# Turning the queries on GpSimd ahead of the token lists, in a fused attention and mixture-of-experts kernel

## The chip, the cores and the metric

One core of a Trainium2 chip runs the whole layer in one launch. The metric is the device time of one execution in microseconds. Engines are named as the profile names them: PE (TensorE), DVE (VectorE), ACT (ScalarE), POOL (GpSimd), SP (SyncE, which only issues DMAs here).

## What is computed

```python
xn = layernorm(x)                                   # x: (8, 256, 256) f32, so 2048 tokens of 256
q, k, v = xn @ Wq + bq, xn @ Wk + bk, xn @ Wv + bv  # 16 heads of 16
q, k = rope(q), rope(k)                             # x*cos + rotated(x)*sin
attn = softmax(causal(q @ k.T / 4)) @ v             # per head, 256 x 256
w, ids = top_k(softmax(xn @ gate.T), 6)             # 64 experts, 6 per token
routed = sum over the 6 of w * down_e(silu(g_e) * u_e)   # FFN width 176
shared = down_s(silu(g_s) * u_s)                    # width 352, all tokens
out = x + attn @ Wo + bo + routed + shared
```

## The kernel before

The program is written engine by engine; the order on each engine is the order of the code, and engines meet only through semaphores. It has four stages, and PE goes through them in this order.

1. Layer norm, transposes, V and router logits (`xn_transpose`, `mix`), then sixteen projections `project(n)` (L1109): four spans of 512 tokens, and in each span two halves of the queries, then two halves of the keys. ACT copies every result out with its bias (`projected`, L560, semaphore `qkv_ok`). Between projections PE computes the ranks of the router, which DVE needs for the slots of every token (L788 to L834; L834 raises `tables_ok`, L788 raises `chosen`).
2. The shared experts on all tokens (`shared_up`, `shared_down`), and beside them the token lists: for each of 16 tiles of tokens DVE writes 12 one-hot tables in fp16 (`one_hot`, L838, two buffers, so at most two tiles ahead) and PE multiplies them (`list_tokens`, L1147). DVE then copies the finished list to `idx_all` (L953, `idx_ok`).
3. The routed experts: 128 tiles of 128 slots, two experts of 64 slots each in a tile, taken two tiles at a time. POOL gathers the rows of a tile by an indirect DMA (`gather`, L450), at most four tiles ahead; PE transposes them (L1168), multiplies up (L1211), transposes (L1222) and multiplies down (L1238). DVE copies the weights of a tile's second expert (`up_copy` L927, `down_copy` L934) and forms the hidden values (L869). SP loads the weights of an expert once its place in a ring of eight is free (L359 to L362).
4. Attention, with the routed results gathered and added beside it.

The change concerns the rotation of queries and keys. Q and K lie in SBUF as pieces: piece n belongs to span n // 2, even n are the queries, odd n the keys. A piece is 128 partitions x 2 halves x 512. It takes nine steps: two products with sin into a spare buffer, two products with cos in place, a subtraction, an addition, a rounded copy, and two differences. Then eight DMAs of 256 KB store it to `qk_rows`, from where stage 4 loads it. In the kernel before, POOL turns the queries (`piece`, L456, steps L481 to L491) and stores queries and keys (L466); DVE turns the keys, one step per pair of tiles in the routed loop (`turn_keys`, L883). All of POOL's steps and stores stand in the routed loop between the gathers, spread evenly by count:

```python
steps = [(n, k) for n in range(PIECES) for k in range(ROPE_STEPS if n % 2 else 0, PIECE_STEPS)]
for r in range(RT):
    gather(r)
    while r >= XB and r % 2 and done < (r - XB + 1) * todo // (RT - 4 * XB) and done < todo:
        piece(*steps[done])
```

Every step of a piece waits for the step ahead of it (`roped`), and the first store of a key piece waits for DVE's ninth step on it (`turned_ok`, L463). There are four spare buffers (`spare`, L230). Number 0 is the space of `raw` and `on`, which the shared experts use for their silu (`gS`, L243), so the first step waits for all shared results (L472). Numbers 1 and 2 lie over router tables, number 3 is free. The fifth and later pieces wait until the stores of the piece four before have landed (`rows_out`, L474 on POOL, L893 on DVE).

Of the kernel before, what the change touches and what calls it, by code (L numbers as in the profile page):

```python
# [35 lines left out]
NT = T // P  # L36
# [12 lines left out]
RT = ((T * TOPK + NE * (GRAIN - 1)) // GRAIN + STRIPS - 1) // STRIPS  # L49
TILES = RT  # L50
XB = 4
# [32 lines left out]
SPAN_T = T // SPANS  # L84
# [7 lines left out]
PIECES = 2 * SPANS  # L92
BUFS = 4
ROPE_STEPS = 9
COPIES = 4
PIECE_STEPS = ROPE_STEPS + 2 * COPIES
# [9 lines left out]
def build(nc, x, wqkv, bqk, bv, bo, wo, wr, wgu, wdn, rope, tri, ident, mask, before, upto, tileno, thr, tok, iota,  # L106
# [7 lines left out]
    with ctx:  # L114
        def sb(name, shape, dt=F32):
            return ctx.enter_context(nc.sbuf_tensor(name, shape, dt))

        def sem(name):
            return ctx.enter_context(nc.semaphore(name))
# [105 lines left out]
        with nc.sbuf_tensor("spare_high", [P, 2, SPAN_T], F32) as spare_high:  # L225
            pass
        raw = sb("raw", [P, 2, S])
        on = sb("on", [P, SB, E])
# [11 lines left out]
        hT = work[0:FP, :, EC * P:(EC + 2) * P].rearrange("p u (k q) -> p u k q", q=P)  # L240
        hS = [[z[:, at * SPAN_T:(at + 1) * SPAN_T] for at in range(2)] + [work[:, u, EC * P:EC * P + SPAN_T]]
              for u, z in enumerate((y.rearrange("p u e -> p (u e)"), freed[0]))]
        gS = [raw[:].rearrange("p u s -> p (u s)"), on[:].rearrange("p s e -> p (s e)")]  # L243
        sg, hid = work[:, :, 4 * P:4 * P + F], work[:, :, 6 * P:6 * P + F]

        wqkv_flat = wqkv_sb[:].rearrange("p c n -> p (c n)")
        own_gu = [wqkv_flat[:, 0:GU].rearrange("p (c n) -> p c n", c=EC),
                  room[:, 1, 0:GU].rearrange("p (c n) -> p c n", c=EC)]
        own_dn = [wqkv_flat[0:FP, GU:GU + DN].rearrange("p (c n) -> p c n", c=2), room[0:FP, 1, GU:GU + DN].rearrange("p (c n) -> p c n", c=2)]
# [26 lines left out]
        tables_ok = sem("tables_ok"); onehot_ok = sem("onehot_ok"); listed = sem("listed"); idx_ok = sem("idx_ok"); dpair = sem("dpair")  # L276
# [50 lines left out]
        order = [(g, k) for g in range(SPANS) for k in range(4)]  # L327
# [107 lines left out]
        @block.gpsimd  # L435
        def _(po):
            po.memset(ones_b[:], 1.0)
            po.memset(ones_c[:], 1.0).then_inc(ones_ok, 1)
            po.memset(v_all[:, :, :, D:2 * D], 1.0).then_inc(pad_ok, 1)
            po.wait_ge(pad_ok, 1)  # L440
            po.memset(work[ROWS[-1]:ROWS[-1] + 1, :, EC * P:EC * P + SPAN_T], 1.0).then_inc(hone_ok, 1)
            po.wait_ge(hone_ok, 1)

            po.wait_ge(c_in_act, 16 * CONSTS)
            for k in range(8):
                a, cs, s = k // 4, k // 2 % 2, k % 2
                last = po.tensor_copy(table_in[:, k], rope_sb[:, s, cs, a, 1::2].unsqueeze(1).to_broadcast([P, H, D // 2]))
            last.then_inc(table_set, 1)

            def gather(r):  # L450
                if r >= XB:
                    po.wait_ge(xt_done, r - XB + 1)
                po.indirect_dma_start(xg[:, r % XB, :], None, xn_rows[:, :],  # L453
                                      bass.IndirectOffsetOnAxis(idx_all[:, r:r + 1], 0)).then_inc(xg_in[r % XB], 16)

            def piece(n, k):  # L456

                g, a, u = n // 2, n % 2, n % BUFS
                q, other = qT[:, g, a], spare[u]
                if k >= ROPE_STEPS:  # L460
                    i, x = (k - ROPE_STEPS) // 2, (k - ROPE_STEPS) % 2
                    if k == ROPE_STEPS:
                        po.wait_ge(turned_ok if a else roped, ROPE_STEPS * (n // 2 + 1))  # L463
                    at = qk_rows.rearrange("(h i x d) a t -> h i d x a t", h=H, i=COPIES, x=2)
                    src = other if i in HIGH_IN[a] else q
                    po.dma_start(at[:, i, :, x, a, g * SPAN_T:(g + 1) * SPAN_T], src[:, x]).then_inc(rows_out[u], 16)  # L466
                    return
                if n or k:
                    po.wait_ge(roped, ROPE_STEPS * (n // 2) + k)
                    po.sem_inc(po_turn, 1)  # L470
                if n == 0 and k == 0:
                    po.wait_ge(sdn_ok, NT)  # L472
                if k == 0 and n >= BUFS:
                    po.wait_ge(rows_out[u], 16 * 2 * COPIES * (n // BUFS))  # L474
                cos, sin = (table[:, a, cs].unsqueeze(1).to_broadcast([P, SPAN_T // S, S]) for cs in range(2))

                def batches(z):
                    return z.rearrange("p (b s) -> p b s", s=S)

                if k < 2:  # L480
                    i = po.tensor_tensor(batches(other[:, k]), batches(q[:, 1 - k]), sin, ALU.mult)  # L481
                elif k < 4:
                    i = po.tensor_tensor(batches(q[:, k - 2]), batches(q[:, k - 2]), cos, ALU.mult)
                elif k == 4:
                    i = po.tensor_tensor(q[:, 0], q[:, 0], other[:, 0], ALU.subtract)
                elif k == 5:
                    i = po.tensor_tensor(q[:, 1], q[:, 1], other[:, 1], ALU.add)
                elif k == 6:
                    i = po.tensor_copy(other.bitcast(F32R), q)
                else:  # L490
                    i = po.tensor_tensor(q[:, k - 7], q[:, k - 7], other[:, k - 7], ALU.subtract)  # L491
                i.then_inc(roped, 1)

            po.wait_ge(qkv_ok, len(order))
            po.wait_ge(tables_in, 1)
            po.wait_ge(idx_ok, 1)
            po.wait_ge(xn_out, 16 * NT)
            steps = [(n, k) for n in range(PIECES) for k in range(ROPE_STEPS if n % 2 else 0, PIECE_STEPS)]
            todo = len(steps)
            done = 0  # L500
            for r in range(RT):
                gather(r)
                while r >= XB and r % 2 and done < (r - XB + 1) * todo // (RT - 4 * XB) and done < todo:
                    piece(*steps[done])
                    done += 1
            assert done == todo

            def rows(t, u):

                for k in range(TOPK):  # L510
                    slot = ROWS_FROM + (TOPK * t + k) * NS // (TOPK * NT)
                    if slot < 0:
                        po.wait_ge(max_ok, slot + AHEAD + 1)
                    else:
                        po.wait_ge(exp_done, slot + 1)
                    if t >= 2:
                        po.wait_ge(dcomb, TOPK * (t - 2) + k + 1)
                    po.indirect_dma_start(yg[u][:, k, :], None, y_rows[:, :],  # L518
                                          bass.IndirectOffsetOnAxis(slot_i[:, t, k:k + 1], 0)).then_inc(yg_in[u], 16)

            po.wait_ge(dn_ok, TILES)
            for s in range(XB):
                po.wait_ge(y_out[s], 16 * (RT // XB))
            for u in range(2):
                rows(u, u)
            for b in range(2, B + 1):
                for s in range(SB):
                    rows(SB * (b - 1) + s, s)
# [936 lines left out]
```

## Time and profile before

| | us |
|---|---|
| median of 3 runs (652.37 to 657.2) | 652.57 |
| the profiled execution | 650.28 |
| its span in the trace | 648.5 |
| PE busy in the span | 621.4 (96%) |
| DVE busy | 437.5 (67%) |
| POOL busy | 321.6 (50%) |

PE's granted clock is full in the whole span. The profiled execution is 1.78 us longer than its span and 2.29 us shorter than the median. In rows of a timeline the columns are the start, the duration, the engine, the line, the operation and what it writes and reads, and in brackets the idle time ahead of it with what ended it. In rows of groups they are the line, the engine, the operation and its shapes, the count, the busy time with the mean in ns, and the idle time ahead.

### The profile page before, as it was taken

How to read it: one execution, taken by the hardware profiler on the slowest of the kernel's cores; microseconds unless marked ns; L12 is line 12 of the kernel's file. 1: busy time of each engine (PE TensorE's matmuls, PEld its weight loads, DVE VectorE, ACT ScalarE, POOL GpSimd, SP SyncE). 2: the span in 40 equal slices, each digit the busy share in tenths (PEclk: the TensorE clock that was granted, in tenths of full speed). 3: DMA queues.
4: the chain of work that ended last, by engine and by line, in shares of the span. 5: the costliest groups of instructions: out<-in, count | busy, mean ns of one | idle time of the engine just before them, and what ended most of it. 6: DMA issues, size and time to landing. Idle time of an engine off the chain costs nothing.

```text
span 648.5 us, 17789 instructions
## 1 busy us (share of the span) xinstructions
PE 621.4 (96%) x4929; PEld 368.7 (57%) x4929; DVE 437.5 (67%) x1364; ACT 306.0 (47%) x798; POOL 321.6 (50%) x340
## 2 busy tenths in 40 slices
PE   7999999999998999999999999999999999999997
PEld 3644455655554555555555555555554666666654
DVE  6768687568665766676665565445446788889865
ACT  3643121024444444444444444445454776777752
POOL 4000000268637766568656776664301766666662
PEclk9999999999999999999999999999999999999999
DMA  9510011138979769995899878995416777877432
GB/s 294 175 37 2 0 34 34 55 85 271 274 243 283 242 190 289 350 304 171 246 310 301 272 230 261 329 271 133 99 50 199 236 218 216 239 218 219 124 105 74
DMA packets 78167, 124.52 MB, mean 192 GB/s; under 512 B 11113, under 2 KB 52618, under 8 KB 78090
## 3 DMA queue, kind: packets, MB, share of 16 engines
q1 hardware_dynamic: 43098, 60.18, 30.4%
q0 software_dynamic: 15872, 46.16, 24.2%
q10 hardware_dynamic: 19120, 17.18, 7.8%
q8 instruction: 45, 0.74, 0.5%
q14 instruction: 32, 0.26, 0.1%
HBM read 85.73 MB, written 37.75 MB: 190 GB/s over the span
## 4 chain that ended last, share of the span: by engine, by line
PE 83%; DVE 5%; DMA 4%; issue 3%; ACT 2%; POOL 2%; DVEq 1%; ACTq 0%; SPq 0%; POOLq 0%
PE pair L1211 23%; PE pair L1238 14%; PE pair L1181 6%; PE pair L1168 5%; PE pair L1116 4%; PE bank L1323 4%; PE bank L1222 3%; PE bank L1195 3%; PE bank L1355 2%; PE pair L1078 2%; PE pair L1278 2%; PE pair L1297 2%; DMA lower<-xn_rows,idx_all 2%; PE pair L1286 2%; DVE negm L980 2%
## 5 line engine op out<-in xcount | busy, mean ns | idle before, releaser
L453 POOL DMA_INDIRECT lower<-xn_rows,idx_all x128 | 139.3, 1089 | 215.0 <-DVE idx_all L953 107.8
L1211 PE MATMUL pair<-space,work 128*64 (+1 forms) x768 | 165.6, 463 | 7.0 <-DVE wqkv_sb L927 3.7
L1238 PE MATMUL pair<-lower,work 88*64 x512 | 122.1, 380 | 1.8 <-ACT lower L614 1.4
L1211 PEld LDWEIGHTS pair<-space,work 128*64 128x64 f32 x768 | 66.8, 137 | 77.7 <-issue 67.2
L869 DVE TENSOR_TENSOR work<-work,pair 128x176 f32<-128x176 f32 x128 | 42.8, 337 | 90.9 <-ACT work L608 90.4
L1238 PEld LDWEIGHTS pair<-lower,work 88*64 88x64 f32 x512 | 69.3, 137 | 50.8 <-issue 20.9
L1211 PE MATMUL pair<-wqkv_sb,work 128*64 128x352 f32 x256 | 89.4, 472 | 0.0
L614 ACT ACTIVATE lower<-pair 128x256 f32<-128x256 f32 x128 | 49.1, 383 | 77.8 <-PE pair L1238 77.8
L518 POOL DMA_INDIRECT wqkv_sb<-y_rows,slot_i x48 | 46.9, 977 | 60.9 <-DVE negm L980 34.0
L980 DVE TENSOR_REDUCE negm<-pair 128x2 f32<-128x256 f32 (+1 forms) x128 | 64.9, 551 | 11.4 <-PE pair L1286 9.9
L659 ACT ACTIVATE pT<-pair 128x768 f32<-128x768 f32 x64 | 51.9, 811 | 42.6 <-PE pair L1309 41.3
L601 ACT ACTIVATE work<-pair 128x256 f32<-128x256 f32 x128 | 42.1, 381 | 62.7 <-PE pair L1168 37.7
L608 ACT ACTIVATE work<-pair 128x176 f32<-128x176 f32 x128 | 41.1, 321 | 57.3 <-PE pair L1211 56.8
L1238 PE MATMUL pair<-space,work 88*64 88x256 f32 x256 | 66.0, 380 | 0.0
L1238 PE MATMUL pair<-wqkv_sb,work 88*64 88x256 f32 x256 | 65.9, 380 | 0.0
L934 DVE COPY space<-lower 88x512 f32 x64 | 35.6, 557 | 31.5 <-issue 30.5
L518 POOL DMA_INDIRECT space<-y_rows,slot_i x48 | 45.8, 954 | 18.4 <-DVE x_all L1024 9.9
L1168 PE MATMUL pair<-id_f,lower 128*128 128x128 f32 x256 | 42.4, 287 | 2.2 <-DMA lower<-xn_rows,idx_all 1.8
L1181 PE MATMUL pair<-space 128*128 128x512 f32 (+1 forms) x96 | 44.4, 596 | 0.0
L622 ACT ACTIVATE work<-bank 88x256 f32<-88x256 f32 x128 | 41.9, 386 | 1.2 <-PE bank L1222 1.2
L1168 PEld LDWEIGHTS pair<-id_f,lower 128*128 128x128 f32 x256 | 27.0, 141 | 27.0 <-issue 24.2
L670 ACT ACTIVATE ring<-qk_all 128x512 fp32r<-128x512 f32 x64 | 39.4, 625 | 1.1 <-ACT lower L614 0.6
(202 smaller groups left out, 1168.6 us busy)
## 6 DMA issues: line engine op xcount, KB each, us to landing
space<-wgu SPq DMA_DIRECT2D x66, 352.0 KB
y_rows<-lower ACTq DMA_DIRECT2D x128, 128.0 KB
qk_all<-qk_rows SPq DMA_DIRECT2D x64, 256.0 KB, 4.2
lower<-wdn SPq DMA_DIRECT2D x64, 176.0 KB
qk_rows<-qk_all POOLq DMA_DIRECT2D x32, 256.0 KB
qk_rows<-space POOLq DMA_DIRECT2D x16, 256.0 KB
xn_rows<-qk_all SPq DMA_DIRECT2D x16, 128.0 KB, 1.8
lower<-xn_rows,idx_all POOLq DMA_INDIRECT x128
```

The costliest lines, as they stand in the source:

```text
L453: po.indirect_dma_start(xg[:, r % XB, :], None, xn_rows[:, :], bass.IndirectOffsetOnAxis(idx_all[:, r:r + 1], 0)).then_inc(xg_in[r % XB], 16)
L518: po.indirect_dma_start(yg[u][:, k, :], None, y_rows[:, :], bass.IndirectOffsetOnAxis(slot_i[:, t, k:k + 1], 0)).then_inc(yg_in[u], 16)
L601: act.activation(xgT[u], bank[u % 2][:, 0:E].rearrange("p (c t) -> p c t", c=EC), ACT.Copy).then_inc(xgT_ok, 1)
L614: act.activation(y[:, u], pair[u % 2][:, 512:512 + E], ACT.Copy).then_inc(y_ok, 1)
L622: act.activation(hT[:, u % 2], bank[2 + u % 2][0:FP, 0:2 * P].rearrange("p (c t) -> p c t", c=2), ACT.Copy).then_inc(hT_ok, 1)
L659: act.activation(pT[:, n % G], pair[1][:].rearrange("p (j k) -> p j k", j=2)[:, :, 0:SPAN], ACT.Exp).then_inc(exp_done, 1)
L869: dve.tensor_tensor(hid[:, u % 2], sg[:, u % 2], pair[u % 2][:, F:2 * F], ALU.mult).then_inc(hid_ok, 1)
L980: last = dve.tensor_reduce(negm[:, qt, m % PAIRS_OF_HEADS], scores[:, :, qt * P:(2 * qt + 1) * P], AX.X, ALU.max, negate=True)
L1168: last = pe.transpose(bank[u % 2][:, c * P:(c + 1) * P], xg[:, u, c * P:(c + 1) * P], id_f[:])
L1181: last = pe.matmul(pair[k % 2][0:ROWS[c], half * SPAN_T:(half + 1) * SPAN_T], wsgu_sb[:, x, at:at + ROWS[c]], xnT[:, TS * span:TS * (span ...
L1211: last = pe.matmul(pair[u % 2][strip, 0:2 * F], xgT[u][:, c, strip], n, start=c == 0, stop=c == EC - 1, skip_group_check=True)
L1238: last = pe.matmul(pair[u % 2][strip, 512:512 + E], hT[:, u % 2, c, strip], n, start=c == 0, stop=c == 1, skip_group_check=True)
```

## The change

POOL now turns and stores all four pieces of queries in one go, before the first gather. Each piece starts when the two projections of its queries have been copied out; the second piece also waits for `tables_ok`, since its spare buffer lies over router tables. Only then comes the wait for the token list and the loop of gathers, in which the 32 stores of the keys are left, one behind every second gather from the 31st on. The silu of the shared experts moves from `raw` and `on` to the projection weights' space. The steps themselves and DVE's part stay.

```diff
-        gS = [raw[:].rearrange("p u s -> p (u s)"), on[:].rearrange("p s e -> p (s e)")]
+        gS = [wqkv_flat[:, u * SPAN_T:(u + 1) * SPAN_T] for u in range(2)]
...
-                if n == 0 and k == 0:
-                    po.wait_ge(sdn_ok, NT)
+                if k == 0:
+                    po.wait_ge(qkv_ok, 4 * g + 2)
+                if n == 2 and k == 0:
+                    po.wait_ge(tables_ok, 1)
...
-            po.wait_ge(qkv_ok, len(order))
             po.wait_ge(tables_in, 1)
+            po.wait_ge(xn_out, 16 * NT)
+            for n in range(0, PIECES, 2):
+                for k in range(PIECE_STEPS):
+                    piece(n, k)
             po.wait_ge(idx_ok, 1)
-            po.wait_ge(xn_out, 16 * NT)
-            steps = [(n, k) for n in range(PIECES) for k in range(ROPE_STEPS if n % 2 else 0, PIECE_STEPS)]
-            todo = len(steps)
+            steps = [(n, k) for n in range(1, PIECES, 2) for k in range(ROPE_STEPS, PIECE_STEPS)]
             done = 0
             for r in range(RT):
                 gather(r)
-                while r >= XB and r % 2 and done < (r - XB + 1) * todo // (RT - 4 * XB) and done < todo:
+                if done < len(steps) and r % 2 and r >= 2 * ROPE_STEPS * (steps[done][0] // 2 + 1) + 3 * XB:
                     piece(*steps[done])
                     done += 1
```

Line numbers in this document are those of the kernel before; behind L471 those of the kernel after are larger by two or three. The order on PE, DVE, ACT and SP stays as it is. On POOL, behind the copies of the rotation tables (L447), the program before goes straight to the gathers (L453, into `lower`), with the first steps of the first piece of queries between them:

```order
L447 COPY lower<-rope_sb 128x128 x8
L453 DMA lower<-xn_rows,idx_all 128x256 x6
L481 ISA
L481 TENSOR_TENSOR spare_high<-qk_all,table 128x512
L453 DMA lower<-xn_rows,idx_all 128x256 x2
L481 TENSOR_TENSOR spare_high<-qk_all,table 128x512
L483 TENSOR_TENSOR qk_all<-qk_all,table 128x512
L453 DMA lower<-xn_rows,idx_all 128x256 x2
```

After the change a whole piece stands there, nine steps and eight stores, and the next one behind it:

```order
L447 COPY lower<-rope_sb 128x128 x8
L483 ISA
L483 TENSOR_TENSOR spare_high<-qk_all,table 128x512 x2
L485 TENSOR_TENSOR qk_all<-qk_all,table 128x512 x2
L487 TENSOR_TENSOR qk_all<-qk_all,spare_high 128x512
L489 TENSOR_TENSOR qk_all<-qk_all,spare_high 128x512
L491 CAST spare_high<-qk_all 128x1024
L493 TENSOR_TENSOR qk_all<-qk_all,spare_high 128x512 x2
L466 DMA qk_rows<-spare_high 16x8x512 x4
L466 DMA qk_rows<-qk_all 16x8x512 x4
L483 TENSOR_TENSOR space<-qk_all,table 128x512 x2
```

So 36 steps and 32 stores moved from between the gathers to the place ahead of them. In the loop, this is how POOL's program before goes on from the last stores of the first queries to the stores of the first keys (`space` is spare buffer 1) and the second queries:

```order
L466 DMA qk_rows<-qk_all 16x8x512
L453 DMA lower<-xn_rows,idx_all 128x256 x2
L466 DMA qk_rows<-space 16x8x512 x2
L453 DMA lower<-xn_rows,idx_all 128x256 x2
L466 DMA qk_rows<-qk_all 16x8x512 x2
L453 DMA lower<-xn_rows,idx_all 128x256 x2
L466 DMA qk_rows<-space 16x8x512 x2
L453 DMA lower<-xn_rows,idx_all 128x256 x2
L466 DMA qk_rows<-qk_all 16x8x512 x2
L453 DMA lower<-xn_rows,idx_all 128x256 x2
L481 TENSOR_TENSOR space<-qk_all,table 128x512
```

And this is the loop after, from its first gather:

```order
L453 DMA lower<-xn_rows,idx_all 128x256 x32
L466 DMA qk_rows<-space 16x8x512
L453 DMA lower<-xn_rows,idx_all 128x256 x2
L466 DMA qk_rows<-space 16x8x512
L453 DMA lower<-xn_rows,idx_all 128x256 x2
L466 DMA qk_rows<-qk_all 16x8x512
L453 DMA lower<-xn_rows,idx_all 128x256 x2
L466 DMA qk_rows<-qk_all 16x8x512
L453 DMA lower<-xn_rows,idx_all 128x256 x2
L466 DMA qk_rows<-space 16x8x512
```

The gathers now run 32 deep with nothing between them, and the first keys' stores stand behind the 32nd gather instead of near the 24th.

## Rows read from the trace of the kernel before

**Rows 1.** The page's slices of the span: POOL's busy tenths in 40 slices.
```profile
POOL 4000000268637766568656776664301766666662
```
**Rows 2.** Busy time by engine in 60 to 120 us: stretch, length, then engines.
```profile
core 0: us, PE busy (x) PEld busy (x) DVE busy (x) ACT busy (x) POOL busy (x), PEclk, DMA share, GB/s
60.00:120.00 60.00, 60.00 (x245) 32.98 (x244) 47.02 (x211) 11.65 (x23) 0.00 (x0) 1.00 0.06 19
```
**Rows 3.** POOL's groups of instructions, shapes kept apart.
```profile
L481 POOL TENSOR_TENSOR space<-qk_all,table 128x512 f32<-128x512 f32 x4 | 5.1, 1286 | 0.1
...
L489 POOL CAST space<-qk_all 128x1024 fp32r<-128x1024 f32 x2 | 2.1, 1036 | 0.3 <-POOL qk_all L487 0.3
...
L466 POOL DMA_DIRECT2D qk_rows<-qk_all x32 | 18.9, 594 | 0.1
```
**Rows 4.** Timelines of ACT, DVE, PE and POOL: what starts and ends stages 1 and 2.
```profile
38.84 0.69 ACT L565 ACTIVATE qk_all<-pair,bias_t 128x512 f32<-128x512 f32 x1 [0.46 <-PE pair L1116]
...
39.84 1.78 DVE L788 TENSOR_TENSOR run_b<-run_b,sel_b 128x64 bf16<-128x64 bf16 x8
...
45.94 0.38 PE L1123 MATMUL pair<-sel_b,tri_b 128*128 128x512 bf16 x1
...
59.53 0.18 DVE L834 TENSOR_SCALAR last_t<-last_c 1x66 int32<-1x66 int32 x1
61.16 0.26 DVE L844 TENSOR_SCALAR is_row<-iota_b,slot_row 128x128 f16<-128x128 f16 x1 [1.45 <-issue]
...
124.28 1.12 POOL L453 DMA_INDIRECT lower<-xn_rows,idx_all  x1 [107.83 <-DVE idx_all L953]
...
133.73 0.60 PE L1168 MATMUL pair<-id_f,lower 128*128 128x128 f32 x4
```
**Rows 5.** Timelines of DVE and POOL early in the routed loop.
```profile
151.08 2.07 DVE L934 COPY wqkv_sb<-lower 88x512 f32 x1
151.57 1.29 POOL L487 TENSOR_TENSOR qk_all<-qk_all,spare_high 128x512 f32<-128x512 f32 x1
153.03 1.04 POOL L489 CAST spare_high<-qk_all 128x1024 fp32r<-128x1024 f32 x1 [0.17 <-POOL qk_all L487]
153.07 1.27 DVE L934 COPY space<-lower 88x512 f32 x1
...
155.51 2.04 POOL L453 DMA_INDIRECT lower<-xn_rows,idx_all  x1 [0.30 <-issue]
...
156.64 0.41 DVE L934 COPY wqkv_sb<-lower 88x512 f32 x1
```
**Rows 6.** DVE's groups of instructions, shapes kept apart: one-hot tables, two f32 tensor_scalars.
```profile
L845 DVE TENSOR_SCALAR is_tile<-iota_b,slot_tile,tok_sb 128x128 f16<-128x128 f16 x96 | 29.2, 304 | 0.0
L844 DVE TENSOR_SCALAR is_row<-iota_b,slot_row 128x128 f16<-128x128 f16 x96 | 23.5, 244 | 1.5 <-issue 1.5
...
L804 DVE TENSOR_SCALAR passed<-passed,cend 64x256 f32<-64x256 f32 x1 | 0.3, 346 | 0.0
L793 DVE TENSOR_SCALAR over<-thr_s,cnt 64x32 f32<-64x32 f32 x1 | 0.2, 231 | 0.0
```
**Rows 7.** PE's busy time in stretches of the routed loop, and in the whole loop.
```profile
154.00:164.00 10.00, 8.29 (x64) 1.00 0.75 213
194.00:204.00 10.00, 7.69 (x58) 1.00 0.83 252
214.00:234.00 20.00, 18.00 (x137) 1.00 0.74 226
284.00:314.00 30.00, 27.35 (x206) 1.00 0.65 196
134.00:484.00 350.00, 339.04 (x2548) 1.00 0.78 239
```
**Rows 8.** The chain that ended last, in the routed loop: start, length, what.
```profile
150.32 6.08 DMA lower<-xn_rows,idx_all
...
196.71 5.88 DMA lower<-xn_rows,idx_all
...
208.02 7.03 DMA lower<-wdn
```

## What the change was predicted to do

> **What bounds the kernel now.** I read the page first, its slices: POOL does nothing from about 16 to 124 us and is then busy for half or more of most slices of the routed loop [rows 1]. That is the hole into which the change puts work. The busy times by stage come next: between 60 and 120 us PE is busy in all 60.00 us and DVE in 47.02 [rows 2]. So the shared experts and token lists are a PE stage with a second engine close behind: DVE has 13.0 us free, and PE waits for nothing. Every microsecond in which DVE's lists come too late is a microsecond of PE.
>
> The routed loop is bound by PE as well: 339.04 of 350 us busy [rows 7]. Its idle 10.96 us stand in a few places. From 154 to 164 PE lacks 1.71 us and from 194 to 204 another 2.31; the chain of waits names gathers there, which took 6.08 and 5.88 us to land behind POOL's late issues [rows 8]. From 214 to 234 and from 284 to 314 it lacks 2.00 and 2.65 us, and the chain shows weights arriving late (7.03 us at 208) [rows 7, 8]. All that better gathers can give back is in these numbers.
>
> **The moved steps on POOL itself.** A piece is eight steps of 1.28 us and a cast of 1.04 [rows 3], each about 0.17 us behind the one ahead, which it waits for [rows 5]: 8 x 1.28 + 1.04 + 8 x 0.17 = 12.6 us. Its eight stores take 8 x 0.59 = 4.7 us of POOL, with the wait ahead of them 4.9, so 17.5 us for a piece. The second half of the first queries is copied out at 39.53, so piece one runs from 39.6 to 57.1. Piece two waits for `tables_ok`, 59.71 [rows 4]; three pieces from there end at 59.7 + 3 x 17.5 = 112.2. The first gather starts at 124.28 now [rows 4]. POOL's own length therefore costs nothing: the wait for the token list covers it with 12 us to spare. The stores meet a nearly idle DMA system (share 0.06 from 60 to 120 us [rows 2]), and the later pieces' spare buffers are long free.
>
> **What stands beside it: DVE.** In the routed loop the two engines meet already. The f32 copy L934 takes 0.41 us when POOL computes nothing. The one at 151.08 took 2.07 us: it ended at 153.15, 0.29 us after POOL's step (151.57 to 152.86). The next one took 1.27 us and ended 0.27 us after POOL's cast [rows 5]. So such a copy does not share with a step of POOL, it stands still for all of it, and one copy fits between two steps. No row shows an fp16 one-hot beside a POOL step. What I can read is how fast they go: the f32 tensor_scalars L793 and L804, which like L844 take one scalar per partition, need 231 and 346 ns for 32 and 256 elements, so 0.51 ns an element and 215 ns fixed. L844 needs 244 ns for 128 elements, 0.23 ns an element [rows 6]. The one-hots are a one-source operation like the copies and go faster still, so I take them as blocked in the same way. That is the choice on which the sign rests.
>
> The Trainium skill, page "SBUF — State Buffer", section "Who interferes with whom", says that DVE and GpSimd share one pair of SBUF ports, that it is an exclusive lock, and that tensor_scalar in its two-port modes takes it as copies do. The copies in [rows 5] agree; for tensor_scalar no row here shows it. By that rule the sum would be the one below.
>
> Now the price. The lists need 192 one-hots; a tile's twelve take about 2.3 us, 0.19 each. From 59.7 on there are three stretches of compute on POOL, 3 x 12.6 = 37.8 us. In each DVE gets what fits into nine gaps. A gap is 0.17 us and the start of the next step, in which the copies found about 0.27 us: two one-hots, so 18 of them or 3.5 us of work. DVE loses 37.8 - 3 x 3.5 = 27.3 us. With one a gap it loses 32.6, with three 22.1. Against that stand 13.0 us of free time [rows 2]. If all of it could be used, 27.3 - 13.0 = 14.3 would reach PE; if none, 27.3. The lists can run only two tiles ahead of PE, so the free time beside the stores cannot all be used; I take about half, 7.3, and get +20. Bounds: 22.1 - 13.0 = +9 and +33.
>
> Piece one meets the router's chain. The eight additions L788 end at 41.62 and PE needs them at 45.94 [rows 4]; at one a gap of 1.45 us they end near 51, at two a gap near 45.6. That is 0 to +5 us, and I take 0, since two a gap is what I took above.
>
> **The routed loop.** Without steps between the gathers the two late gathers go: 1.71 + 2.31 = 4.0 us. Of the 4.65 us of late weights I take half, 2.3: 32 stores of 256 KB leave the loop, but the loads still start only when a slot is freed. DVE's blocked copies go too; PE saw them inside the same idle time. So -6, bounds -11 (all idle) and 0. One thing is new: a key store waits for its turn, and DVE's first step on the third piece of keys waits for the landing of the first piece's stores. Those are issued behind gathers 31 to 45, up to 14 gathers later than now. DVE's step stands behind tile pair 38; gather 45 is issued when PE begins pair 36. That leaves about two pairs, 10 us, for an issue of some 3 us and a landing like the gathers' 6 us [rows 8]. Queued behind that DVE step are the weight copies of the next pair, for which PE waits. I take 0; up to 4 us each for the third and fourth pieces is the upper bound, so the loop's range is -11 to +8.
>
> **Sum.** Against the profiled execution: 650.28 + 20 - 6 = 664.3. The median of the runs lies 2.29 us higher, so 666.6; forecast 666 us. Its own range is 654 to 682.
>
> **Rivals.** *The lists go past POOL.* If the fp16 one-hots are not blocked, only f32 copies and operations with two SBUF inputs (the router's chain, which has slack) meet POOL before 124 us. Then stage 2 keeps its length, and the loop's gain is all there is: 652.6 - 6 = 646.6, with 641.6 at best. This is the case on the other side. For it speaks that the one-hots hold their data path for only about 0.03 us each (244 against 215 ns fixed); against it that no copy which met a POOL step in [rows 5] got past it. It decides at whether DVE's one-hots begin inside POOL steps: if more than about six of them fit for each POOL step, 27 x 6 x 0.19 = 31 us of DVE's work, the loss disappears.
>
> *DVE wins instead.* At 155.51 a gather of POOL took 2.04 us instead of the 1.12 of the first one, behind copies of DVE that followed each other [rows 4, 5]. If the one-hots hold off POOL in the same way, the lists are on time and POOL is late: 27 steps each waiting for half a tile's twelve, 1.15 us, add 31 us, so the pieces end at 143 and the first gather is issued 19 us late. PE starts on the first tiles at 133.73, and a gather issued at 124.28 lands at about 130.4, so 3.3 us are covered: 652.6 + 15.7 - 6 = 662. The same page of the Trainium skill, in that section, says that the order of issue, not the kind of operation, decides who blocks; by that rule this case and the forecast are both open, and the trace shows both orders.
>
> *The loop gains nothing.* Weights arrive as late as before and gathers become late elsewhere: this only moves the forecast to 672 and lies in its range.
>
> **Chances.** Blocked lists 0.68, lists that pass 0.20, POOL held off 0.12. A difference of 1% (6.5 us) is about what a measurement of this kernel can tell. Blocked lists give slower by over 1% in 0.60, within 1% in 0.06, faster in 0.02. Passing lists lie around 646.6, just at the 1% line: 0.12 faster, 0.08 within. POOL held off: 0.10 slower, 0.02 within. Together 0.14, 0.16 and 0.70. The range from 646 to 682 leaves out the better half of the passing lists and the one-a-gap end of the blocked ones.
>
> **What would show it.** Right: between 60 and 120 us PE's busy time falls by 10 us or more, PE waits for DVE's L844 and L845, these stretch to more than 1 us when POOL computes, and the first gather comes near 144 instead of 124.28. The loop then takes about 6 us less from its first transpose to its last. Wrong: L844 and L845 keep 244 and 304 ns beside POOL and PE stays full until 133 (lists that pass); or the first gather is released by POOL's own last store (POOL held off); or DVE's key step behind pair 38 waits for the stores, which would make the loop longer.

## The result, and the profile after

The changed kernel takes 665.53 us (median of 4 runs, 662.95 to 666.12) beside 652.81 for the kernel before in the same runs: a ratio of 1.0181, 95% interval 1.015 to 1.0213, so it is slower by 1.8%. The forecast was 666. In the profiled executions (662.95 and 650.28 us) the spans differ by 661.1 - 648.5 = 12.6 us, and two rows of PE's timeline say where they come from: the first transpose of a routed tile (133.73 before, [rows 4]), and the last group of four of these transposes. First the kernel after, then the kernel before:

```profile
157.80 0.60 PE L1171 MATMUL pair<-id_f,lower 128*128 128x128 f32 x4
...
485.26 0.66 PE L1171 MATMUL pair<-id_f,lower 128*128 128x128 f32 x4
```

```profile
472.61 0.66 PE L1168 MATMUL pair<-id_f,lower 128*128 128x128 f32 x4
```

The stage of the shared experts and lists ends 24.1 us later. From there to the last transposes it takes 327.5 us instead of 338.9, 11.4 less, and what follows is as long as it was. So +24 and -11, not the +20 and -6 of the prediction.

The page of the kernel after, POOL's slices and PE's granted clock, to be read against [rows 1]:

```profile
POOL 3056897004333444455444555443300766666662
PEclk9999887999999999999999999999999999999999
```

POOL now works in the third to seventh slices. The clock, full everywhere before, dips in the same place. The busy times of 60 to 120 us answer to [rows 2]:

```profile
core 0: us, PE busy (x) PEld busy (x) DVE busy (x) ACT busy (x) POOL busy (x), PEclk, DMA share, GB/s
60.00:120.00 60.00, 42.79 (x140) 20.39 (x139) 56.92 (x139) 9.27 (x19) 46.17 (x51) 0.86 0.39 124
```

PE has lost 17.2 us of a stretch that was full, and DVE, which had 13.0 us free, is busy nearly throughout. What PE waited for between 40 and 158 us (total, times, longest):

```profile
PE pair L1153 <- DVE is_tile L848: 17.2, 6, 4.9
PE bank L1147 <- DVE passed L807: 0.2, 1, 0.2
```

The other 6.7 of the 24.1 us are busy time of PE, whose matmuls took longer at the lower clock; the run on the clock below takes that up.

And this is how DVE's one-hots look beside POOL's steps (DVE's and POOL's timelines, from the first one-hot on):

```profile
62.46 1.27 POOL L483 TENSOR_TENSOR space<-qk_all,table 128x512 f32<-128x512 f32 x1 [4.82 <-DVE last_t L837]
63.76 0.25 DVE L847 TENSOR_SCALAR is_row<-iota_b,slot_row 128x128 f16<-128x128 f16 x1 [1.46 <-issue]
63.91 1.27 POOL L483 TENSOR_TENSOR space<-qk_all,table 128x512 f32<-128x512 f32 x1 [0.18 <-POOL space L483]
63.93 1.29 DVE L848 TENSOR_SCALAR is_tile<-iota_b,slot_tile,tok_sb 128x128 f16<-128x128 f16 x1
65.15 0.24 DVE L847 TENSOR_SCALAR is_row<-iota_b,slot_row 128x128 f16<-128x128 f16 x1
65.31 1.36 DVE L848 TENSOR_SCALAR is_tile<-iota_b,slot_tile,tok_sb 128x128 f16<-128x128 f16 x1
...
147.67 1.04 POOL L453 DMA_INDIRECT lower<-xn_rows,idx_all  x1 [33.88 <-DVE idx_all L956]
```

The L848 at 63.93 was issued inside POOL's step (63.91 to 65.18) and ended at 65.22, when the step was over; the L847 behind it went through at its usual 0.24, and the next L848 met the next step. Two one-hots for each step of POOL, as the sum had assumed. The last row is the first gather, 23.4 us later than in [rows 4], and released by DVE's list, not by POOL.

Not every operation of DVE is held: these two, later in the same trace, each read one operand from SBUF as f32 and one from PSUM, run inside a step of POOL and take what they take elsewhere (0.68 and 0.42 us on average):

```profile
103.94 1.27 POOL L489 TENSOR_TENSOR qk_all<-qk_all,space 128x512 f32<-128x512 f32 x1 [0.18 <-POOL qk_all L487]
103.95 0.67 DVE L861 TENSOR_TENSOR space<-wqkv_sb,pair 128x512 f32<-128x512 f32 x1
104.55 0.41 DVE L866 TENSOR_TENSOR x_all<-x_all,bank 128x256 f32<-128x256 f32 x1
```

In the routed loop PE's idle stretches are gone. These windows answer to [rows 7]; the first one falls at the loop's start here, the last one is the loop:

```profile
154.00:164.00 10.00, 8.69 (x51) 1.00 0.34 102
194.00:204.00 10.00, 10.00 (x80) 1.00 0.65 198
214.00:234.00 20.00, 20.00 (x154) 1.00 0.76 220
284.00:314.00 30.00, 30.00 (x228) 1.00 0.88 269
158.00:484.00 326.00, 324.55 (x2454) 1.00 0.77 228
```

### The profile page after: what moved, and what is told of

It is laid out like the page before. It is cut to its first block, busy times and chain, and to the rows that moved or that the text cites. A ratio compares the mean times of both kernels' runs of the same rounds, so it can differ in the third digit from the quotient of the medians.

```text
span 661.1 us, 17791 instructions
## 1 busy us (share of the span) xinstructions
PE 625.2 (95%) x4929; PEld 369.4 (56%) x4929; DVE 455.4 (69%) x1364; ACT 305.3 (46%) x798; POOL 314.2 (48%) x340
## 4 chain that ended last, share of the span: by engine, by line
PE 80%; DVE 14%; ACT 3%; issue 2%; DMA 0%; DVEq 0%; ACTq 0%
PE pair L1214 24%; PE pair L1241 17%; PE pair L1171 6%; PE bank L1225 4%; PE bank L1326 4%; PE pair L1184 4%; DVE is_tile L848 3%; PE bank L1198 3%; DVE is_row L847 3%; PE bank L1358 2%; PE pair L1081 2%; PE pair L1281 2%; PE pair L1300 2%; DVE negm L983 2%; PE pair L1119 2%
## 5 line engine op out<-in xcount | busy, mean ns | idle before, releaser
L453 POOL DMA_INDIRECT lower<-xn_rows,idx_all x128 | 133.4, 1042 | 211.7 <-PE pair L1171 158.0
L983 DVE TENSOR_REDUCE negm<-pair 128x2 f32<-128x256 f32 (+1 forms) x128 | 64.9, 550 | 11.4 <-PE pair L1289 10.2
L1184 PE MATMUL pair<-space 128*128 128x512 f32 (+1 forms) x96 | 49.3, 652 | 0.0
L937 DVE COPY space<-lower 88x512 f32 x64 | 30.0, 469 | 21.9 <-issue 20.9
L848 DVE TENSOR_SCALAR is_tile<-iota_b,slot_tile,tok_sb 128x128 f16<-128x128 f16 x96 | 41.6, 434 | 0.0
```

The costliest lines, as they stand in the source:

```text
L848: last = dve.tensor_scalar(is_tile[:, u, k], iota_b[:], slot_tile[:, t, k:k + 1], tok_sb[:, t:t + 1], ALU.is_equal, ALU.mult)
L983: last = dve.tensor_reduce(negm[:, qt, m % PAIRS_OF_HEADS], scores[:, :, qt * P:(2 * qt + 1) * P], AX.X, ALU.max, negate=True)
L1184: last = pe.matmul(pair[k % 2][0:ROWS[c], half * SPAN_T:(half + 1) * SPAN_T], wsgu_sb[:, x, at:at + ROWS[c]], xnT[:, TS * span:TS * (span ...
```

## The experiments

The theory: DVE's one-hots stand still while POOL turns the queries, and PE waits for the lists. The rivals: the stores and their traffic are to blame; any operation of DVE is held; or the lower clock is a cost of its own. For the loop: its gain comes from the place of the steps, from their pacing, or from the stores' traffic. "Rest" below is the span from the first transpose on, which was 648.5 - 133.73 = 514.8 us before.

**The stores alone.** The 27 steps of pieces two to four are left out, and their stores write queries that are not turned (they read the pieces themselves and wait for `qkv_ok` and `tables_ok` in place of the steps).

```diff
...
-                for k in range(PIECE_STEPS):
+                for k in range(ROPE_STEPS if n else 0, PIECE_STEPS):
                     piece(n, k)
```

> The kernel after without POOL's 27 turning steps on the second, third and fourth pieces of queries; their 24 stores stay, and store queries that are not turned. Theory (DVE's one-hots stand still during POOL's steps): with the steps gone the lists are on time, the first gather comes at 124 to 128 us, PE does not wait for the one-hots (under 2 us between 60 and 120 us), its clock stays full, and the time is about 665.5 - 24 = 641 us. Rival (the stores' descriptors or traffic beside the lists cost the time): the first gather stays near 147 us and the time near 660 to 666.

It took 638.84 us (one run, span 637.0). Timelines of POOL, DVE and PE:

```profile
62.88 12.69 POOL L472 DMA_DIRECT2D qk_rows<-qk_all  x24 [5.21 <-DVE last_t L843]
63.78 0.25 DVE L853 TENSOR_SCALAR is_row<-iota_b,slot_row 128x128 f16<-128x128 f16 x1 [1.46 <-issue]
63.95 0.31 DVE L854 TENSOR_SCALAR is_tile<-iota_b,slot_tile,tok_sb 128x128 f16<-128x128 f16 x1
...
123.68 1.03 POOL L453 DMA_INDIRECT lower<-xn_rows,idx_all  x1 [48.12 <-DVE idx_all L962]
...
133.81 0.60 PE L1177 MATMUL pair<-id_f,lower 128*128 128x128 f32 x4
```

All 24 stores are issued beside one-hots of the usual 0.25 and 0.31 us, and the stage ends where it did before the change. The steps cost the 24 us, the stores by themselves nothing. One detail stays open: in the kernel after, two one-hots that were issued during the last stores of a piece (at 78.47 and 95.65) stood until the first step of the next piece was over, 2.47 and 2.40 us, and no run says why they were held before that step's row begins. The rest is 503.2 us, the same as in the kernel after (503.3).

**The one-hots' input in PSUM.** The row of numbers is copied once to an unused PSUM bank as f32, and the one-hots read it from there.

```diff
...
-                    dve.tensor_scalar(is_row[:, u, k], iota_b[:], slot_row[:, t, k:k + 1], None, ALU.is_equal)
+                    dve.tensor_scalar(is_row[:, u, k], iota_p, slot_row[:, t, k:k + 1], None, ALU.is_equal)
...
```

> The kernel after, with the one-hots reading their row of numbers as f32 from PSUM instead of as fp16 from SBUF. Theory (what is blocked is the operand's way from SBUF, which POOL shares): beside POOL the one-hots no longer stretch; each is slower by itself by 0.07 to 0.1 us, 192 of them 13 to 19 us against 13 us of free DVE time, so the first gather comes at 125 to 132 us and the time is 642 to 650 us. Rival (any operation of DVE waits while POOL computes): they stretch to over 1.2 us as before, the first gather comes at 150 us or later and the time is 666 to 672.

It took 654.34 us, ratio to before 1.0008 (0.9988 to 1.0027). DVE's groups:

```profile
L851 DVE TENSOR_SCALAR is_tile<-pair,slot_tile,tok_sb 128x128 f16<-128x128 f32 x96 | 38.5, 401 | 0.0
L850 DVE TENSOR_SCALAR is_row<-pair,slot_row 128x128 f16<-128x128 f32 x96 | 32.8, 342 | 1.7 <-issue 1.7
```

Over all 96 executions L850 stays between 336 and 351 ns, though POOL makes the same steps beside it. So it is not DVE as a whole that is held, but the one-hot in the form that reads its row as fp16 from SBUF. The run changes the place and the type of the row, and with them the speed, all at once, so it does not say which of these counts; that an operand comes from SBUF is not enough by itself, as L861 and L866 above show. On the page "SBUF — State Buffer" (section "Who interferes with whom") the Trainium skill says that a DVE instruction with at most one SBUF input, outside the two-port modes, does not meet GpSimd; this trace agrees. The time lies between what theory and rival had said, and the first gather (137.88) comes later than the theory's 125 to 132: the one-hots are slower by 98 and 97 ns each, 18.7 us together, and of these 14.3 reached PE (first transpose at 148.01). I had expected 13 us of free DVE time to swallow most of it.

**One piece ahead.** Only the first piece stays ahead; the others go into the loop, one step or store behind every second gather.

```diff
-            for n in range(0, PIECES, 2):
-                for k in range(PIECE_STEPS):
-                    piece(n, k)
+            for k in range(PIECE_STEPS):
+                piece(0, k)
+            turns = [(n, k) for n in range(2, PIECES, 2) for k in range(PIECE_STEPS)]
...
                 gather(r)
+                if r >= XB and r % 2 and turns:
+                    piece(*turns.pop(0))
```

> The kernel after, with only the first piece of queries ahead; the other three are turned and stored in the routed loop, one step or store behind every second gather, the keys' stores where the change put them. Theory (three pieces beside the lists cost 8 us each, the first one nothing): first gather at 124 us, first transpose at about 134; the loop keeps part of its gain, 6 to 10 of 11.5 us, since steps again meet DVE's copies; time 643 to 648 us. Rival (the loop gains only because the steps and query stores are gone from it): the loop takes as long as before and the time is 651 to 654.

642.49 us, ratio 0.9833 (0.9802 to 0.9864): faster than both kernels, and just below the 643 to 648 of its theory. The first piece meets only the router's chain and costs 0.3 us (first transpose at 134.02). PE's windows in the loop, as in [rows 7]:

```profile
154.00:164.00 10.00, 10.00 (x78) 1.00 0.81 236
194.00:204.00 10.00, 9.69 (x73) 1.00 0.88 248
214.00:234.00 20.00, 19.97 (x154) 1.00 0.92 297
284.00:314.00 30.00, 30.00 (x228) 1.00 0.95 300
134.00:484.00 350.00, 346.41 (x2606) 1.00 0.77 235
```

Its 3.59 us of idle time stand against 10.96 before. The rest is 506.6 us.

**The clock.** Between the list products at which PE waited stand idle matmuls that keep it at work.

```diff
+            IDLE = {0: 12, 1: 3, 2: 20, 3: 9, 5: 17, 6: 8}
...
+                if t in IDLE:
+                    keep_on(bank[1][:], IDLE[t])
                 pe.wait_ge(onehot_ok, t + 1)
```

> The kernel after, with 69 idle matmuls of PE (0.2 us each, into an unused bank) placed ahead of the six list products at which PE waits for the one-hots. In the kernel after the granted clock falls to 0.66 of full in three stretches of 10 us there, and the matmuls that ran then took about 6 us more. Theory (the lower clock is a cost of its own beside the waits): clock full throughout, time 659 to 662 us. Rival (PE would only wait longer for DVE, which sets the pace in these stretches): 664 to 667.

663.25 us, ratio 1.0154 (1.012 to 1.0187). The interval overlaps that of the kernel after. The window of 60 to 120 us for PE (its width, busy time and instructions, granted clock, DMA share and GB/s):

```profile
60.00:120.00 60.00, 53.39 (x209) 0.97 0.39 125
```

And in PE's timeline the first transpose, with its start:

```profile
158.22 0.60 PE L1177 MATMUL pair<-id_f,lower 128*128 128x128 f32 x4
```

The mean granted clock of the stretch is 0.97 instead of 0.86, but the stage ends at 158.22, not earlier than 157.80. So in the trace the rival holds: DVE sets the pace there (it is busy in all of 70 to 110 us in both kernels), and a PE that computes faster mostly waits longer. But the time lies between the two forecasts, and 2.3 us below the median of the kernel after, which was taken in other runs. The stage's end differs by as much between runs of one program: in the run with more stores below, whose program is the same up to the first gathers, it comes at 159.67. So the 4 to 6 us of the theory are not there; whether the lower clock costs up to about 2 us stays open.

**All pieces in the loop, paced.** Nothing is ahead; one step or two stores follow every second gather.

```diff
...
+            for n in range(0, PIECES, 2):
+                turns += [[(n, k)] for k in range(ROPE_STEPS)]
+                turns += [[(n, ROPE_STEPS + 2 * k), (n, ROPE_STEPS + 2 * k + 1)] for k in range(COPIES)]
...
```

> The kernel after with all four pieces of queries turned and stored in the routed loop again, but paced: one step, or two stores, behind every second gather from the sixth to about the 108th, the keys' stores where the change put them. Theory (the routed loop of before lost its 11 us to the order, namely several steps at once between early gathers and a key store that waits for DVE, and not to where the queries are turned): first transpose at 133.7, loop as in the version with one piece ahead (8 us shorter than before), time 643 to 646 us. Rival (the gain of the loop comes from steps and query stores having left it): 650 to 653.

647.61 us, ratio 0.9923 (0.9901 to 0.9944): between the two. The rest is 645.1 - 134.13 = 511.0 us, 3.8 less than before, not 8. In the four stretches of [rows 7] pacing gives back nearly all, PE lacks 0.97 us there instead of 8.67; but other waits came elsewhere, and in the whole loop it lacks 6.09 instead of 10.96:

```profile
154.00:164.00 10.00, 10.00 (x80) 1.00 0.82 244
194.00:204.00 10.00, 9.35 (x71) 1.00 0.94 290
214.00:234.00 20.00, 19.80 (x154) 1.00 0.87 265
284.00:314.00 30.00, 29.88 (x230) 1.00 0.85 253
134.00:484.00 350.00, 343.91 (x2573) 1.00 0.78 239
```

**More stores in the loop.** The kernel after with 32 more stores of 256 KB.

```diff
...
                 gather(r)
+                if r >= 5 and r % 2 and extra:
+                    again(extra.pop(0))
```

> The kernel after with 32 more stores of 256 KB each, from the query pieces to a buffer in device memory that nothing reads, one behind every second gather from the sixth to the 68th. Theory (weights arrived late in the loop of before because gathers and steps were late, not because of the stores' traffic): the loop stays within 1 us of the kernel after, time 664.5 to 667. Rival (the traffic of the query stores makes the weights late): the loop is 3 to 6 us longer, 668 to 672.

665.74 us, ratio 1.02 (1.0178 to 1.0223); the rest is 663.2 - 159.67 = 503.5 us, against 503.3 in the kernel after. Stores alone, without the steps, do not lengthen the loop.

**The second piece beside the lists, spread out, and in one go.** In the first version each step waits for one more finished list tile:

```diff
...
+            for k in range(PIECE_STEPS):
+                if k < ROPE_STEPS:
+                    po.wait_ge(listed, k + 2)
+                piece(2, k)
...
```

> The version with one piece ahead (642.5 us), with the second piece turned beside the lists, but only one step for each finished list tile, from the second to the tenth. Theory (a step costs DVE one stop of 1.1 us, and DVE has 13 us free there, so nine stops spread over nine tiles are absorbed): first gather within 2 us of 124, the loop a little shorter, time 640 to 644 us. Rival (each stop reaches PE in full, since the lists run close ahead of it): first gather 8 to 10 us later, time 650 to 653.

> The version with one piece ahead, with the second piece ahead as well, its nine steps in one go. Theory (each piece turned beside the lists costs about a third of the 24 us that three of them cost): first gather near 131.5, first transpose near 142, time 648 to 651 us. Rival (the free time of DVE takes up a single piece, so that the cost is not proportional): first gather at 124 to 127 and time 641 to 645.

Spread out: 645.58 us, ratio 0.9886 (0.9865 to 0.9908). In one go: 647.19 us (one run), just below the 648 to 651 of its theory. Their first gathers:

```profile
128.70 1.05 POOL L453 DMA_INDIRECT lower<-xn_rows,idx_all  x1 [20.12 <-DVE idx_all L962]
```

```profile
130.46 1.04 POOL L453 DMA_INDIRECT lower<-xn_rows,idx_all  x1 [50.47 <-DVE idx_all L959]
```

The first transposes come at 138.83 and 140.58, so nine steps cost 4.8 us when spread and 6.6 in one go, beside one piece ahead at 134.02. Spreading helps little: it cost half of what its rival said and was far from free. The price is roughly proportional, 6.6 us for one piece and 24.1, or 8.0 each, for three; DVE's free time did not take up a single piece.

The rest over all versions, by how many steps of POOL are left in the loop:

| steps in the loop | version | rest, us |
|---|---|---|
| 36, several at once | before | 514.8 |
| 36, paced | nothing ahead | 511.0 |
| 27 | one ahead | 506.6 |
| 18 | two ahead, in one go; spread | 504.8; 506.4 |
| 0 | after; steps left out; idle matmuls; more stores; input in PSUM | 503.3; 503.2; 503.3; 503.5; 504.7 |

These are single profiles, and versions with the same number of steps differ by up to 1.6 us, so 18 and 27 steps cannot be told apart here.

## Why the prediction was right

**POOL's own length, right.** Its last step was to end with the stores at 112.2 us; the stores end at 113.8, because the router's chain raised `tables_ok` 2.6 us later and the pieces were a little shorter. The first gather still waits for DVE's list.

**The one-hots are blocked, right, and of the size that was worked out.** Two for each step, and DVE was to lose 27.3 us. DVE's groups after, against [rows 6]:

```profile
L848 DVE TENSOR_SCALAR is_tile<-iota_b,slot_tile,tok_sb 128x128 f16<-128x128 f16 x96 | 41.6, 434 | 0.0
L847 DVE TENSOR_SCALAR is_row<-iota_b,slot_row 128x128 f16<-128x128 f16 x96 | 38.7, 403 | 1.5 <-issue 1.5
```

96 x (434 - 304 + 403 - 244) = 27.7 us. The inference from their speed held, and the runs without steps and with the PSUM input show the cause from both sides. The Trainium skill (page "SBUF — State Buffer", section "Who interferes with whom") says that tensor_scalar, in its two-port modes, can contend with GpSimd as copies can. These rows agree (244 to 403 ns and 304 to 434), though no row shows the mode.

**"I take about half" of DVE's free 13.0 us, mis-sized.** 24.1 of the 27.7 lost us reached PE, so 3.6 were absorbed, not 7.3. The other runs say the same: of the 18.7 us that the PSUM input added, 4.4 were absorbed, though nothing was held there. With two buffers DVE can run two tiles ahead, and of its 13.0 us the trace of the kernel before names 7.7 as waiting for PE. That the buffers are why so little was absorbed is argued; no run varied their number.

**The loop's -6, mis-sized: it was -11.4.** The late gathers went, as forecast. What the prediction called late weights went in full, where it took half since "32 stores of 256 KB leave the loop"; that reason was wrong, since 32 stores put back changed nothing. The name was wrong too, at least in part. What PE waited for in the loop of the kernel before (total, times, longest), and one of these waits:

```profile
PE pair L1211 <- DVE wqkv_sb L927: 3.7, 6, 0.9
PE pair L1168 <- DMA lower<-xn_rows,idx_all: 1.8, 2, 1.6
```

```profile
223.63 1.27 POOL L485 TENSOR_TENSOR qk_all<-qk_all,space 128x512 f32<-128x512 f32 x1 [0.18 <-POOL qk_all L483]
223.85 1.12 DVE L879 SCALAR_TENSOR_TENSOR sel_b<-space,top 128x64 f32<-128x64 f32 x1
...
225.72 0.51 DVE L927 COPY wqkv_sb<-space 128x704 f32 x1
...
226.64 0.51 PE L1211 MATMUL pair<-space,work 128*64 x1 [0.67 <-DVE wqkv_sb L927]
```

All of the 2.00 us that PE lacks between 214 and 234 is waiting for such copies. Here DVE's operation L879, with two inputs in SBUF, took 1.12 us beside POOL's step (0.28 at 212.36), the copy behind it came that much later, and PE waited 0.67. So here a step of POOL reached PE through DVE, and the list of PE's waits after the change has no such copy left. How the rest of the gain divides between held operations of DVE and gathers issued late behind steps, the runs do not separate. The table shows that the loop shortens as steps leave it and, by 3.8 us, with their pacing; not in proportion, since the first nine to leave gave 4.4 us and the other 27 only 3.3, and the pacing was not the same in both. The bound of -11, "all idle", was passed by a little: PE's idle time between the first and the last transposes fell from 10.96 to 1.45 us, and its busy time by 1.9. The new wait of the key stores cost nothing.

**The router's chain, 0 of 0 to +5, right**: L791, L788 before, took 5.73 us instead of 1.78 and was done at 45.36, before PE asked for it at 45.72.

The errors were about 4 and 5 us and of opposite sign, so the sum of +14 met +12.6. The forecast is good in its mechanism; that it came within 2 us is luck, since either error alone would have put it 4 to 5 us off. Its range, 654 to 682, is also narrower than its bounds add up to (about 651 to 694 around the median). Of the rivals, the lists did not go past POOL, and DVE did not hold POOL off: all 27 steps beside the lists took 1.26 to 1.28 us, the casts 1.04.

## What to carry to other kernels

An idle GpSimd is not free room: before moving its steps, list which operations VectorE runs there and find a row that shows each kind beside a GpSimd step. Here f32 copies and fp16 tensor_scalars that read SBUF alone stood still, as did operations with two SBUF inputs, while those with one of two inputs from PSUM ran on. Count one stop of a whole GpSimd step for every gap, into which only two small operations fit. Free time of the second engine in a tightly coupled pair can be worth little (here 3.6 of 13 us). Move the part that has no such neighbour and pace the rest: one piece ahead of the lists and single steps between gathers gave 642.49 us, where all pieces ahead cost 13.

## What was not expected of the hardware

The granted clock fell in three stretches of ten us (means 0.83, 0.66 and 0.66 of 2.4 GHz, so partly at 1.2) where PE waited for the lists; matmuls of the shared experts there took 0.71 us each instead of 0.45 (eight in 5.71 us, 3.60 before). Yet holding the clock up did not bring the end of the stage forward in the profiles, because DVE was what the stage waited for; up to about 2 us stays open.

POOL can be the one that waits. One step of its first piece took 2.03 us, beside DVE's product of 1024 elements, which also took 2.18 instead of 1.23 (timelines of POOL and DVE):

```profile
49.41 1.27 POOL L493 TENSOR_TENSOR qk_all<-qk_all,spare_high 128x512 f32<-128x512 f32 x1 [0.18 <-POOL spare_high L491]
49.58 2.18 DVE L803 TENSOR_TENSOR space<-space,sel_b 128x1024 f32<-128x1024 f32 x1
50.85 2.03 POOL L493 TENSOR_TENSOR qk_all<-qk_all,spare_high 128x512 f32<-128x512 f32 x1 [0.18 <-POOL qk_all L493]
51.79 2.17 DVE L804 TENSOR_TENSOR space<-space,wsum 128x1024 f32<-128x1024 f32 x1
```

DVE's operation was held until POOL's step ended at 50.68, ran about 1.1 us, and POOL's next step, issued at 50.85, then took its 1.27 us from about 51.6 on. Here they took turns, one whole operation each; beside the lists POOL never waited.
